# Stacked attention keys of one batch element: fetched by one transfer with a zero-stride source, spilled together, key pieces ahead of value pieces

## What is computed

```
x = x + L0_xattn(norm(x), ctx, mask)     # attention over 375 context rows, keys = values = ctx, one head
x = x + L0_ffn(norm(x), w1, w2, w3)      # ternary weights, 8-bit activations, 512 -> 1408 -> 512
x = x + L1_xattn(norm(x), ctx, mask)     # 16 heads of 32: q from x; k, v = ctx @ Wk.T + bk, ctx @ Wv.T + bv
x = x + L1_ffn(norm(x), integer weights) # 512 -> 1408 -> 512
```

## Time and profile before

| | |
|---|---|
| median of 3 runs | 618.28 us |
| profiled execution | 617.85 us, its span 616.1 us |
| TensorE busy | 496.8 us (81%) |
| VectorE, ScalarE, GpSimd busy | 321.1, 237.3, 84.8 us |
| moved by DMA | 79.30 MB in 31,005 packets |
| stacked keys fetched (`kst`) | 32 transfers of 384 KB, median 7.1 us from issue to landing |
| keys spilled (`k_scratch`) | 128 transfers of 48 KB, median 1.8 us |

### The profile page before, as it was taken

The page is one execution under the profiler, slowest core; times in us unless marked ns, Lnnn a source line. Parts: engine busy times, 40 slices in busy tenths (PEclk is TensorE's granted clock), DMA queues, the critical chain, the costliest instruction groups (busy, mean ns, idle before and its releaser), DMA issues. The chain is left out here.

```text
span 616.1 us, 10094 instructions
## 1 busy us (share of the span) xinstructions
PE 496.8 (81%) x3954; PEld 373.5 (61%) x3954; DVE 321.1 (52%) x529; ACT 237.3 (39%) x351; POOL 84.8 (14%) x68
## 2 busy tenths in 40 slices
PE   3799999975968799998597655556667749999997
PEld 3678778763845566665395554445556525555797
DVE  5734375324656756555432414644468996555411
ACT  3334533441374455555535534334431325222100
POOL 3200040003304000000200000000008534000000
PEclk9799999988889899999697966788887889999999
DMA  8986659523370211100676945666605122000011
GB/s 266 403 308 192 199 152 316 175 96 92 138 266 17 85 42 55 48 30 31 172 175 145 283 114 132 155 154 155 155 3 201 82 75 113 0 2 0 15 46 60
DMA packets 31005, 79.30 MB, mean 129 GB/s; under 512 B 5745, under 2 KB 19057, under 8 KB 27889
## 3 DMA queue, kind: packets, MB, share of 16 engines
q1 hardware_dynamic: 30960, 78.69, 41.6%
q10 hardware_dynamic: 2, 0.01, 0.0%
HBM read 58.76 MB, written 14.42 MB: 119 GB/s over the span
## 5 line engine op out<-in xcount | busy, mean ns | idle before, releaser
L167 PE MATMUL psum<-wv_p,kv_p 128*128 128x512 f32 x288 | 80.0, 429 | 7.6 <-DVE wv_p L620 4.3
L165 PE MATMUL psum<-kv_p,wk_p 128*128 128x384 f32 x384 | 76.5, 352 | 11.5 <-PEq L665 7.3
L1334 ACT ACTIVATE e<-psum,mask_bias 128x448 f32<-128x448 f32 x96 | 53.7, 634 | 66.6 <-PE psum L1355 66.5
L165 PEld LDWEIGHTS psum<-kv_p,wk_p 128*128 128x128 f32 x384 | 69.7, 196 | 13.9 <-issue 9.5
L1355 PE MATMUL psum<-qst,kst 128*128 128x112 f16 x384 | 32.1, 249 | 49.0 <-DMA kst<-k_scratch 45.1
L167 PEld LDWEIGHTS psum<-wv_p,kv_p 128*128 128x128 f32 x288 | 56.8, 200 | 24.5 <-issue 12.2
L1390 DVE TENSOR_SCALAR e<-e 128x1344 f32<-128x1344 f32 x32 | 27.4, 858 | 73.4 <-ACT e L1334 73.4
L1355 PEld LDWEIGHTS psum<-qst,kst 128*128 128x128 f16 x384 | 25.4, 117 | 56.7 <-DMA kst<-k_scratch 46.5
L1369 PE MATMUL psum<-e,vst 128*32 128x112 f32 x768 | 41.4, 293 | 2.2 <-DVE e L1390 2.2
L1736 PE MATMUL psum<-xt,wg_b 128*128 128x448 f16 x176 | 38.4, 363 | 5.0 <-DVEq L1781 5.0
L187 DVE SCALAR_TENSOR_TENSOR khl<-psum,bqk,khl 128x384 f16<-128x384 f32 x32 | 19.7, 614 | 42.8 <-ACT khl L177 42.6
(11 more groups left out here) (176 smaller groups left out, 849.0 us busy)
## 6 DMA issues: line engine op xcount, KB each, us to landing
kst<-k_scratch SPq DMA_DIRECT2D x32, 384.0 KB, 7.1
kv_raw<-in_ctx_feat SPq DMA_DIRECT2D x12, 768.0 KB, 5.2
w_stage<-in_w SPq DMA_DIRECT2D x6, 1408.0 KB, 7.3
cn<-in_ctx_tok SPq DMA_DIRECT2D x8, 768.0 KB, 6.4
k_scratch<-khl SPq DMA_DIRECT2D x128, 48.0 KB, 1.8
v_scratch<-vsp SPq DMA_DIRECT2D x24, 256.0 KB, 2.0
vst<-v_scratch SPq DMA_DIRECT2D x8, 768.0 KB, 10.7
w_int<-in_wg SPq DMA_DIRECT2D x2, 1408.0 KB, 8.8
```

Source lines behind the costliest of these rows:

```text
L165: mm = pe.matmul(psum[:, kv_bank(p), 0:TP], wk_p[:, u, k, n * P:(n + 1) * P], src[:, v, k, :], **ends)
L167: mm = pe.matmul(psum[:, kv_bank(p), :], src[:, u, k, n * P:(n + 1) * P], wv_p[:, v, k, :], **ends)
L1334: act.activation(e[g][:, c, :], psum[:, D_S + (TC * g + c) % 4, 0:4 * S], ACT.Exp, bias=mask_bias[:, b, c:c + 1]).then_inc(e_raw, 1)
```

## The change

1. The keys of an element lie in one tile `khl` (high and low, four groups of heads) and in HBM as (2, 32, 4 heads of a group, groups and rows); they are spilled by four transfers once the last keys piece has been read, with one semaphore `k_spilled` for all. A piece other than the last issues no spill.
2. A fetch of stacked keys is one transfer: the destination has all 128 partitions, the source is (2, 64, 3072) float32 with a stride of zero on the 2. The bytes are the same.
3. `kst` has its two middle dimensions in the other order.
4. Within an element the four keys pieces come first, then the three values pieces. The split of the values' weights and the reads of the pieces are moved to fit.

```diff
-        PIECES = (("k", 0), ("k", 1), ("v", 0), ("k", 2), ("v", 1), ("k", 3), ("v", 2))
+        PIECES = (("k", 0), ("k", 1), ("k", 2), ("k", 3), ("v", 0), ("v", 1), ("v", 2))
...
-        khl = [at(f"khl{g}", [P, 2, TP], F16, 195456 + g * 1536) for g in range(G)]
+        khl = at("khl", [P, 2, G, TP], F16, 195456)
...
-        k_scratch = nc.dram_tensor("k_scratch", (B, 2, HD, G, 4, TP), F16).ap()
+        k_scratch = nc.dram_tensor("k_scratch", (B, 2, HD, 4, G * TP // 2), F32).ap()
...
-        k_spilled = [sem(f"k_spilled{g}") for g in range(G)]
+        k_spilled = sem("k_spilled")
...
-                after(act, k_spilled[n], 64 * i)
+                after(act, k_spilled, 64 * i)
...
-            kv_wait_read(sp, p)
-            if kind == "k":
+            if kind == "v":
+                kv_wait_read(sp, p)
+                sp.dma_start(v_scratch[b, :, n], vsp[:, n]).then_inc(v_spilled[n], 16)
+            elif n == G - 1:
+                kv_wait_read(sp, p)
                 for hh in range(4):
-                    sp.dma_start(k_scratch[b, :, :, n, hh].rearrange("u d t -> d u t"),
-                                 khl[n][32 * hh:32 * hh + 32]).then_inc(k_spilled[n], 16)
-            else:
-                sp.dma_start(v_scratch[b, :, n], vsp[:, n]).then_inc(v_spilled[n], 16)
+                    sp.dma_start(k_scratch[b].rearrange("u d h x -> h d u x")[hh],
+                                 khl[32 * hh:32 * hh + 32].bitcast(F32).rearrange("d u g t -> d u (g t)")).then_inc(k_spilled, 16)
...
-        kst = [at(f"kst{q}", [P, G, 4, TP], F16, 123136 + q * 12288) for q in range(2)]
+        kst = [at(f"kst{q}", [P, 4, G, TP], F16, 123136 + q * 12288) for q in range(2)]
...
-            for c in range(4):
-                sp.dma_start(kst[q][32 * c:32 * c + 32], k_scratch[b, c % 2]).then_inc(kst_loaded[q], 16)
+            sp.dma_start(kst[q][:].bitcast(F32).rearrange("p h g t -> p (h g t)"),
+                         k_scratch[b:b + 1].rearrange("o u d h x -> o (u d) (h x)")
+                         .to_broadcast([2, 2 * HD, 4 * G * TP // 2])).then_inc(kst_loaded[q], 16)
...
             exponentials(0)
-            projection_high(1, wv_p, wv_raw)
             act.wait_ge(keys_bias, 16 * 3)
...
             kv_read_hi(act, 3)
+            projection_high(1, wv_p, wv_raw)
...
             kv_read_lo(dve, 0)
-            projection_low(1, wv_p, wv_raw)
...
+            kv_read_lo(dve, 2)
             kv_read_lo(dve, 3)
+            projection_low(1, wv_p, wv_raw)
...
-                    pe.wait_ge(kst_loaded[q], 64 * (b // 2 + 1))
+                    pe.wait_ge(kst_loaded[q], 16 * (b // 2 + 1))
```

More of the change, by code:

```diff
@@ L175, in kv_read_hi @@
             if kind == "k":
-                after(act, k_spilled[n], 64 * i)
-                act.activation(khl[n][:, 0, :], psum[:, kv_bank(p), 0:TP], ACT.Identity,
+                after(act, k_spilled, 64 * i)
+                act.activation(khl[:, 0, n, :], psum[:, kv_bank(p), 0:TP], ACT.Identity,
                                bias=bqk[:, 1, n:n + 1]).then_inc(kv_hi, 1)
@@ L186, in kv_read_lo @@
                 dve.wait_ge(kv_hi, p + 1)
-                dve.scalar_tensor_tensor(khl[n][:, 1, :], psum[:, kv_bank(p), 0:TP], bqk[:, 1, n:n + 1], khl[n][:, 0, :],
+                dve.scalar_tensor_tensor(khl[:, 1, n, :], psum[:, kv_bank(p), 0:TP], bqk[:, 1, n:n + 1], khl[:, 0, n, :],
                                          ALU.add, ALU.subtract).then_inc(kv_left, 1)
@@ L755, in _ @@
                     load_feat(i + 2)
-            for g in range(G):
-                sp.wait_ge(k_spilled[g], 64 * B)
+            sp.wait_ge(k_spilled, 64 * B)
             for c in range(TC):
@@ L1354, in scores @@
                     for hh in range(4):
-                        mm = pe.matmul(psum[:, D_S + (TC * g + c) % 4, hh * S:(hh + 1) * S], kst[q][:, g, hh, c * P:(c + 1) * P],
+                        mm = pe.matmul(psum[:, D_S + (TC * g + c) % 4, hh * S:(hh + 1) * S], kst[q][:, hh, g, c * P:(c + 1) * P],
                                        qst[:, g, hh, b * S:(b + 1) * S], start=True, stop=True)
```

## The result

The changed kernel takes 803.69 us (median, 802.58 to 805.80) against 618.67, the median of four runs of the kernel before: the ratio is 1.2998, with a 95% interval from 1.2961 to 1.3036. The profiled execution has a span of 804.1 us, 188.0 more than before.

A forecast was written before the change was run, and what follows sets the result against it. The prediction took the kernel as bound by a loop of key-fetch latency plus 6.3 us; 135 (stage D) + 40 (stage C) + 5 (start) = +180 us on 617.85 gave 798 us, range 770 to 835.

The forecast's parts named there:

- The bound: TensorE waits 45.1 us in six for stacked keys; fetch latency plus 6.3 us loops without slack, so changes count six times.
- Stage D: Score matmuls with six key fetches in the loop, each 22.5 us longer: +135 us.
- Two of 16 engines, 30.0 us of data: Each key fetch runs on 2 of 16 DMA engines: 30.0 us in place of 7.5, +22.5 us per fetch.
- Stage C: First two key fetches, hidden before, delay the query transfers behind them, so TensorE starts scores at 370.7, not 330.67: +40 us.
- the bound of +12: If SyncE cannot issue query transfers ahead while the two engines' queues are full: up to 12 us more.
- The start, +5: New order of pieces: values' weights are split later, first values piece at 33.1: +5 us, bounds 0 and 6.
- Small edits, nothing: Fewer spill issues, one spill semaphore, keys alternating between banks: nothing, in stage B's single-bank stretches up to 2 us either way.
- rival A: Key fetch on all 16 engines at full 26.2 GB/s each: faster, 588 to 606 us; chance 9%.
- the rule of 60/n us: Key fetch data take 60/n us on n engines; at n = 8 as long as before, above it the change pays.

The follow-up runs named there:

- the run that mends it: Changed kernel with four fetches, SyncE writing in stage B the unfinished element's keys ahead of the last ternary weights' load: 617.08 us, against 628.10 with four fetches alone.
- (64, 2, row): Kernel before with a one-transfer key fetch, zero stride as second dimension, queries laid out to fit: 596.55 us; the same on the changed kernel: 603.27 us.
- n = 8: Kernel before with one fetch whose source is 16 rows read eight times, zero stride in front: 680.26 us, ratio 1.1006.
- n = 16: Kernel before with one fetch whose source is 8 rows read sixteen times, zero stride in front: 617.81 us, ratio 0.9998.
- (16, 8, row): Kernel before with one fetch of 128 different rows as sixteen runs of eight, without a zero stride: 619.91 us, ratio 1.0033.

## Why the prediction was right, point by point

- **The bound.** Right. Stage D is a loop of fetch latency plus 6.3 us, and every fetch's loss stood in the time six times: +135.2 us, with +135 forecast.
- **Two of 16 engines, 30.0 us of data.** Right: share 0.13, 53 GB/s, issue to resume 33.2 and 33.0 in two fetches, with 33 forecast. What carried it was reading the access pattern as the instruction has it. The shares of 0.13, 0.25, 0.52 and 0.96 show the number of engines at outermost counts of 2, 4, 8 and 16; by the rule of the Trainium skill ("DMA: Bandwidth & Descriptors", the section on why a DMA increments its semaphore by 16) it would be just that.
- **Stage C, +40.** +40.8. SyncE's first `qst` issue moved from 318.16 to 339.27, but the issues went on as the transfers ahead drained, and the second keys fetch held the two engines meanwhile (share 0.12 from 356 to 364 us). Nothing of the bound of +12 came.
- **The start, +5.** +6.2. The chain has the order that was worked out, but its parts were sized partly by luck. The first values piece was put at 33.1 and began at 35.33: VectorE's statistics ahead of it began 1.4 us later in this execution (17.40 against 15.96), when x had landed, and the third keys piece, after a wait of 3.48 us, ran at a granted clock of 0.50 and took 4.18 us. Later steps were shorter than summed (4.59 for the first values piece, not 5.3). And only about 4 of the 6.2 are the split, to which the sum gave all; 1.9 remained with the split early.
- **Small edits, nothing.** This step failed. "A spill lands in 1.8 us" is a median over all spills and says nothing of one behind loads, and the step left out what SyncE must do before it can issue the spill. In stage B that is a wait for VectorE and 2.5 MB of loads. The joint semaphore turns this into a stop of 8.5 us, worth 10 us at the first key fetch and 11 in the whole by the run that mends it. That it stands as only +5.1 in the sum here is luck: the rest of the change makes stage B 5.8 us shorter, which the step did not have either.
- **The rate in rival A.** Right for the form that one would write, (64, 2, row). But the rule of 60/n us, with the fetch as long as before at n = 8, is wrong: issue to resume was 18.8 us at n = 8, and at n = 16 it was 10.7, so that nothing was gained. An engine's 26.2 GB/s was taken for every transfer over 128 partitions, and with 4, 8 and 16 in front it moved 13.3 to 15.3. (The smallest wait for keys in the kernel before is 5.55 us, at 428.43, not the 6.05 that was read; it is still above the 3.7.)
- **The total.** 798 forecast, 803.69 measured. The profiled execution took 805.80, 8.0 over the sum of 797.9: 5.1 for the spill, 1.2 at the start, 1.0 in stages C and D, 0.7 after them.

## What to carry to other kernels

Read the outermost counts of both sides of a transfer as the instruction carries them, before its bytes: a repeat belongs inside, behind a dimension with many rows, and if the order of partitions is free, the partner operand can be laid out to allow it. That all engines work is not enough: (16, 8, row) kept sixteen busy at half the rate, and only a trial of the shape showed it. When several buffers come to share one semaphore, look up where in the issuing queue the last of their transfers stands and what it waits behind; the median landing time tells nothing of that. A transfer on a few engines can also hold up the issue of what stands behind it in the queue: 28.73 us for one issue behind two engines; behind four it was 0.92, but the 32 `qst` issues still took 48.72 in place of 23.62.

## What the runs showed of the hardware that I had not expected

- An engine moves some 26 GB/s or about half of it (13.1 to 13.7; 15.3 with four engines), and which of the two does not follow from the number of partitions alone: 128 partitions in one transfer had 13.4 with (16, 8, row) and 25.9 with (64, 2, row).
- SyncE's issue of a 768 KB transfer took 28.73 us behind two key fetches on two engines. That fourteen engines stood idle (share 0.13 from 328 to 336 us) did not help.
- Two engines moved 26.5 GB/s each while every one of 64 rows was read twice; reading a row twice cost nothing there, nor with (64, 2, row) at 25.9.
- After a wait of 4.08 us TensorE's granted clock was 1.00 in one kernel and 0.50 in another.
